# Rope by accumulating transfers, all taps of v on VectorE, and two pairs of tiles for the folded squares

## The reference

```
q, k, v = conv4(silu(xn @ Wq)), conv4(silu(xn @ Wk)), conv4(silu(xn @ Wv))   # causal, 4 taps per channel
z, a, b = xn @ Wz, xn @ Wa, xn @ Wb
q = q * cos + rot_half(q) * sin          # rot_half([u1, u2]) = [-u2, u1]; the same for k
q, k = q / |q|, k / |k|
out = sum over s in 0..3 of (q . lag(k, s)) * scale * sigmoid(lag(a, s) * b) * lag(v, s)
out = out * rsqrt(mean(out^2)) * norm_w * silu(z)
y = x + (out @ Wout) * silu(ffn(xn))     # ffn: sign weights, relu, 2048 hidden units
```

## Time and profile before

| | |
|---|---|
| time, median of 3 runs (lowest to highest) | 1356.13 us (1355.78 to 1356.19) |
| the profiled execution's own time | 1355.53 us |
| its span, first to last instruction | 1353.7 us |
| mean granted TensorE clock, as a share of full speed | 0.998 |
| busy: PE, DVE, ACT, POOL | 1318.3, 982.0, 784.5, 485.1 us |

### The profile page before, as it was taken

How to read it: one execution, slowest core, us unless ns; L and a number is a source line. 1 busy time by engine, 2 the same in 40 slices (tenths; PEclk the granted TensorE clock), 3 DMA queues, 4 the chain that set the end, 5 groups by cost and what they waited for, 6 DMA issues and landing times. The chain is left out here.

```text
span 1353.7 us, 22528 instructions
## 1 busy us (share of the span) xinstructions
PE 1318.3 (97%) x6568; PEld 1103.8 (82%) x6568; DVE 982.0 (73%) x1531; ACT 784.5 (58%) x1504; POOL 485.1 (36%) x634
## 2 busy tenths in 40 slices
PE   6999999999999999999999999999999999999998
PEld 5688888888888888888888888887888888888886
DVE  7889999999999999999999999996122223334342
ACT  5666676767766666666666676766543444422221
POOL 6245454545545455555555454553000000000001
PEclk9999999999999999999999999999999999999999
DMA  8366656666566566665666656555710101156543
GB/s 262 81 131 127 134 116 151 133 130 136 120 146 135 124 132 134 140 141 121 130 144 121 147 119 139 123 118 137 243 40 24 47 15 55 50 184 203 170 133 139
DMA packets 141562, 171.83 MB, mean 127 GB/s; under 512 B 32720, under 2 KB 69584, under 8 KB 141264
## 3 DMA queue, kind: packets, MB, share of 16 engines
q1 hardware_dynamic: 114160, 121.48, 32.0%
q0 software_dynamic: 27360, 49.82, 21.6%
HBM read 62.58 MB, written 25.30 MB: 65 GB/s over the span
## 5 line engine op out<-in xcount | busy, mean ns | idle before, releaser
L1254 DVE TENSOR_TENSOR hid_lo<-relu,hid_hi 128x512 fp32r<-128x512 f32 x64 | 44.3, 692 | 169.1 <-ACT hid_hi L1246 169.1
L798 DVE SCALAR_TENSOR_TENSOR y_k<-u_k,cw_k,y_k 128x512 f32<-128x512 f32 x192 | 146.1, 761 | 27.4 <-ACT y_k L651 20.6
L798 DVE SCALAR_TENSOR_TENSOR y_q<-u_q,cw_q,y_q 128x512 f32<-128x512 f32 x192 | 144.4, 752 | 22.5 <-ACT y_q L651 14.8
L1346 POOL TENSOR_TENSOR g_buf<-g_buf,up_raw 128x512 f32<-128x512 f32 x3 | 3.8, 1279 | 356.2 <-DVE g_buf L1406 356.2
L510 POOL TENSOR_TENSOR rnorm<-norms,neg_half 128x8 f32<-128x8 f32 x64 | 122.6, 1915 | 9.5 <-POOL norms L506 8.5
L1242 ACT ACTIVATE relu<-bank,us_sb 128x512 f32<-128x512 f32 x64 | 44.1, 690 | 123.3 <-PE bank L1265 123.3
L540 POOL DMA_DIRECT2D sq_sum<-out_sq x62 | 53.9, 869 | 162.4 <-DVE norms L831 112.4
L1366 ACT ACTIVATE hid_hi<-o_raw 128x512 fp32r<-128x512 f32 x64 | 40.2, 630 | 116.0 <-PE bank L1475 97.3
L1426 DVE TENSOR_TENSOR hid_lo<-o_raw,hid_hi 128x512 fp32r<-128x512 f32 x64 | 43.8, 690 | 79.9 <-ACT hid_hi L1366 79.9
L690 ACT ACTIVATE down_raw<-y_q 64x512 f32<-64x512 f32 x64 | 40.5, 632 | 103.3 <-PE bank L1036 103.3
L526 POOL TENSOR_TENSOR rq_win<-rq_win,const 128x32 f32<-128x32 f32 x64 | 30.1, 471 | 194.9 <-DMA rq_win<-rq_scratch 194.9
(11 more groups left out here) (193 smaller groups left out, 3711.8 us busy)
## 6 DMA issues: line engine op xcount, KB each, us to landing
swapped_q<-y_q SPq DMA_DIRECT2D x128, 128.0 KB, 2.4
swapped_k<-y_k SPq DMA_DIRECT2D x128, 128.0 KB, 2.4
o_scratch<-o_buf SPq DMA_DIRECT2D x64, 256.0 KB, 3.4
o_raw<-o_scratch SPq DMA_DIRECT2D x64, 256.0 KB, 4.0
down_raw<-down_raw POOLq DMA_DIRECT2D x63, 256.0 KB, 3.4
y_v<-down_raw POOLq DMA_DIRECT2D x63, 256.0 KB, 4.3
sq_sum<-out_sq POOLq DMA_DIRECT2D x62, 256.0 KB, 3.3
raw_q<-in_wq SPq DMA_DIRECT2D x16, 256.0 KB, 3.1
```

The source lines that it names most:

```text
L798: nc.vector.scalar_tensor_tensor(y[n][:, g % 2, :], u[n][:, g % 2, i:i + CH], cw[n][:, bass.ds(h * TAPS + i, 1)], y[n][:, g % 2, :], ALU.m ...
L1254: nc.vector.tensor_tensor(hid_lo[:, j % HS, :], relu[:, j % 2, :], hid_hi[:, j % HS, :].bitcast(fp32), ALU.subtract).then_inc(hid_lo_done, 1)
```

## The change

- **Rope.** `rope(n, i)` now has two operations instead of three. `i = 0` is `y * cos` into `rot` as before; `i = 1` multiplies `y`, not a swapped copy of it, with a sine table of opposite signs, into `swapped`. The four plain copies by SP (two each for q and k) are gone. In their place POOL's `add_swapped(n)` issues two half-height DMAs for each of q and k, which carry each half of `swapped` to the other half of `rot` and add it there. `score` waits for their landing (`rope_added`).
- **v.** The third tap of v is DVE's (line 798) in every step; ACT's last tap (line 654) and POOL's `add_last_tap` are gone, and `turn_v` waits for DVE's third tap.
- **Squares.** `fold` and `other` are two tiles each, taken by g % 2, so that ACT's squares wait for `turned_f` = c-1. POOL waits for the fold before.
- **Order.** On DVE the rope of k is one step late and stands among the taps of q; `gate_scores` and `mask_band` stand between taps 2 and 3 of k; `join_out` and `make_o` among the taps of v; the three splits are spread. On ACT silu of v comes ahead of the squares of q, and the squares of k at the end of the step. On POOL the step begins `fold_squares`, `add_swapped("q")`, `add_swapped("k")`, and then `make_gates` and the rest as before.

```
         def step(h, g):                       # POOL
             c = h * G + g
             if at := back(h, g, 1):
-                fold_squares(c)
-                add_last_tap(at[1], c)
+                fold_squares(at[1], c)
+                add_swapped("q", at[1], c - 1)
+                add_swapped("k", at[1], c - 1)
             if at := back(h, g, 3):
                 make_gates(at[1], c - 3)
...
-        def fold_squares(c):
+        def fold_squares(g1, c):
             wait(pool, squares_done, c)
+            wait(pool, folded, 16 * (c - 1))
             pool.sem_inc(fold_asked, 1)
-            nc.gpsimd.dma_start(fold, other, accum_op=ALU.add).then_inc(folded, 16)
+            nc.gpsimd.dma_start(fold[g1 % 2], other[g1 % 2], accum_op=ALU.add).then_inc(folded, 16)
+
+        def add_swapped(n, g1, k):
+            wait(pool, rope_done[n], 2 * (k + 1))
+            pool.sem_inc(rope_asked, 1)
+            for to, frm in ((0, HALF), (HALF, 0)):
+                nc.gpsimd.dma_start(rot[n][to:to + HALF, cols(g1)], swapped[n][frm:frm + HALF, g1 % 2, :],
+                                    accum_op=ALU.add).then_inc(rope_added[n][g1 % 2], 16)
...
     def step(h, g):                           # ACT
             if not is_start(h, g):
                 silu_and_tap("q", bank_qv, h, g, c)
+            if back(h, g, 4):
+                square_out(c - 4)
+            if not is_start(h, g):
                 silu_and_tap("k", bank_kz, h, g, c)
             if g == 3 and not is_last(h):
                 split_hi("q", h + 1, c)
-            squares("q", g, c)
-            if back(h, g, 4):
-                square_out(c - 4)
             silu_and_tap("v", bank_qv, h, g, c)
             if g == 3 and not is_last(h):
                 split_hi("k", h + 1, c)
-                split_hi("v", h + 1, c)
-            squares("k", g, c)
+            squares("q", g, c)
...                                            # silu of z, copy of v, save_spill
+            squares("k", g, c)
+            if g == 3 and not is_last(h):
+                split_hi("v", h + 1, c)
...
     def step(h, g):                           # DVE, after
             conv_tap("q", 1, h, g, c)
             if at1: rope("k", 0, at1[1], c - 1)
             conv_tap("q", 2, h, g, c)
             if at1: rope("k", 1, at1[1], c - 1)
             conv_tap("q", 3, h, g, c)
             conv_tap("k", 1, h, g, c)
             if at1: sum_fold(at1[1], c)
             conv_tap("k", 2, h, g, c)
             if at3: gate_scores(at3[1], c - 3); mask_band(at3[1], c - 3)
             conv_tap("k", 3, h, g, c)
             if g == 3 and not is_last(h): split_lo("q", h + 1)
             conv_tap("v", 1, h, g, c)
             rope("q", 0, g, c)
             conv_tap("v", 2, h, g, c)
             if at3: join_out(at3[1], c)
             conv_tap("v", 3, h, g, c)
             if g == 3 and not is_last(h): split_lo("k", h + 1)
             if at3: make_o(at3[0], at3[1], c - 3)
             rope("q", 1, g, c)
             if g == 3 and not is_last(h): split_lo("v", h + 1)
...
     def turn_v(g1, c):                        # PE
-            wait(pe, last_tap_added, 16 * c)
+            wait(pe, conv_done["v"], 3 * c)
...
     def score(g2, k):
-            wait(pe, rope_done["q"], 3 * (k + 1 + ahead))
-            wait(pe, rope_done["k"], 3 * (k + 1))
+            wait_rope(pe, "k", g2, k)
+            wait_rope(pe, "q", g2, k)
+            if ahead:
+                wait_rope(pe, "q", g2 + 1, k + 1)
```

More of the change, by code:

```diff
@@ L324, in attention, with wait_rope @@
     sq_asked = sem("sq_asked")
[L325 to L330, removed]
+    DVE_TAPS = {"q": 3, "k": 3, "v": 3}
+    fold, other = ([down_raw[:, i, j, :] for i in range(2)] for j in range(2))
+    def wait_rope(eng, n, g, c):
+        wait(eng, rope_added[n][g % 2], 32 * (c // 2 + 1) if isinstance(c, int) else
+             c * 16 + (32 if g % 2 == 0 else 16))
     def back(h, g, k):
@@ L570, in on_gpsimd @@
         schedule(pool, step)
+        for n in "qk":
+            add_swapped(n, G - 1, NC - 1)
         roots(H - 1, G - 1, NC)
@@ L688, in squares @@
             wait(act, conv_done[n], 3 * c + 3)
[L689 to L691 removed]
+            wait(act, turned_f, c - 1)
+            nc.scalar.activation(fold[g % 2][own, :], y[n][own, g % 2, :], ACT.Square)
+            last = nc.scalar.activation(other[g % 2][own, :], y[n][far, g % 2, :], ACT.Square)
             if n == "k":
@@ L730, in step @@
                 save_spill(at[1], c)
+            squares("k", g, c)
+            if g == 3 and not is_last(h):
+                split_hi("v", h + 1, c)
+            elif g == 3:
+                for n in "qkvz":
+                    act.wait_ge(wlo_done[n], H)
+                ffn.up_signs(0)
+                ffn.up_signs(1)
             if g == 1 and not (isinstance(h, int) and h == 0):
@@ L862, in step @@
             c = h * G + g
-            for n in "qk":
-                for i in (1, 2, 3):
-                    conv_tap(n, i, h, g, c)
+            at1, at3 = back(h, g, 1), back(h, g, 3)
+            conv_tap("q", 1, h, g, c)
+            if at1:
+                rope("k", 0, at1[1], c - 1)
+            conv_tap("q", 2, h, g, c)
+            if at1:
+                rope("k", 1, at1[1], c - 1)
+            conv_tap("q", 3, h, g, c)
+            conv_tap("k", 1, h, g, c)
+            if at1:
+                sum_fold(at1[1], c)
+            conv_tap("k", 2, h, g, c)
+            if at3:
+                gate_scores(at3[1], c - 3)
+                mask_band(at3[1], c - 3)
+            conv_tap("k", 3, h, g, c)
             if is_start(h, g):
@@ L883, in step @@
                         ALU.mult).then_inc(prod_done, 1)
[L884 to L889, removed]
+            if g == 3 and not is_last(h):
+                split_lo("q", h + 1)
+            conv_tap("v", 1, h, g, c)
             if is_start(h, g):
@@ L892, in step @@
             rope("q", 0, g, c)
[L893 to L896, removed]
             conv_tap("v", 2, h, g, c)
[L898 to L901, removed]
+            if at3:
+                join_out(at3[1], c)
+            conv_tap("v", 3, h, g, c)
             if g == 3 and not is_last(h):
                 split_lo("k", h + 1)
+            if at3:
+                make_o(at3[0], at3[1], c - 3)
+            rope("q", 1, g, c)
+            if is_end(h, g):
+                dve.wait_ge(squares_done, NC)
+                nc.vector.tensor_tensor(fold[g % 2], fold[g % 2], other[g % 2], ALU.add).then_inc(folded_last, 1)
+            if g == 3 and not is_last(h):
                 split_lo("v", h + 1)
-            for i in (1, 2):
-                rope("q", i, g, c)
-                rope("k", i, g, c)
             if is_start(h, g - 1):
```

94 lines of the change are left out of this document (39 added, 55 removed).

## The result

The changed kernel takes **1375.63 us** (median of 4 runs, 1375.57 to 1376.10) against 1355.95 for the kernel before in the same session (4 runs, 1353.48 to 1356.19): a ratio of 1.0150, with a 95% interval of 1.0132 to 1.0168. It is 1.5% slower; I had said 1351, 0.4% faster. The time lies in the stated range, but inside rival 2's 1369 to 1377 and on the other side of the kernel before from my case. The profiled execution took 1376.1, its span is 1374.3.

A forecast was written before the change was run, and what follows sets the result against it. PE, busy 97% of the span, was taken as the bound. Against 1355.5: - 16.0 (head stalls) + 13.8 (steps) - 2.0 (end) - 0.5 (start) = - 4.7, so 1350.8, stated as 1351 us; range 1336 to 1376.

The forecast's parts named there:

- rival 2: New stall outweighs gain: half-height DMA over 0.76 on POOL, 0.52 to 0.66 lost a step, 1369 to 1377; chance 0.28.
- my case: Head stalls won, PE loses 0.23 us in each step: 1351 us, 0.4% faster, spread 1346 to 1357; chance 0.43.
- d: POOL's time for one half-height DMA, bounded by 0.44 and 0.92 us, taken as 0.66; same result from 0.62 to 0.76.
- T + 11.72: Latest harmless end of mask_band in us, T being the step's start; PE loses nothing if every step meets it.
- heads and steps: Steps 3 to 62: 16.0 us of head stalls won, 60 x 0.23 = 13.8 lost to late gates.
- the start: Silu of v no longer waits in step 1; a gain of 0.5 us, since the next fold waits for other things.
- the end: Wait for silu of z (2.09) and slow clock (1.7) go, last fold and gates cost some; gain taken as 2 us.
- DVE's new order: DVE's operations timed within a step: mask_band ends at 11.61 us after its start if gates are there, 0.11 before the limit.
- the 16.0 us of the heads: Time lost in steps 3 to 62, mostly PE's sum_values waiting for coefficients once per head; all to be won.
- Three taps of v in DVE's idle time: The third tap of v on DVE costs nothing while 1.8 us are free in a step; otherwise 0.66 a step.
- a POOL operation waits for DVE's work on two tiles: POOL's third gates operation, beside tap 2 of k on DVE, waits for the tap's end and ends at 10.36 us.
- silu of v no longer waits in step 1: At the start, ACT's silu of v ahead of the squares removes a wait; taken as 0.5 us gained.

The follow-up runs named there:

- gates_first: The changed kernel with make_gates moved on POOL ahead of the half-height transfers of k: 1341.54 us, ratio to the kernel before 0.9903.
- v_two_taps: gates_first with the last tap of v left out altogether, so its output lacks that tap: 1337.73 us, ratio to the kernel before 0.9879.
- ends_too: gates_first with split_lo of k earlier on DVE, step 2's fold before step 1's key gates, third last chunk's gates before the last roots: 1336.64 us.
- three_pieces: The changed kernel with each rope half's 128 rows moved in three accumulating transfers (32, 32, 64) instead of two of 64: 1405.90 us, ratio to before 1.0385.

## Why the prediction was wrong

**The failed step** is the one that I called d, "the half-height DMA is not in the trace ... I take the middle, 0.66". It measured 0.81 (32 rows 0.77, 128 rows 0.85). The bounds 0.44 to 0.92 held it; the choice between them did not. It lies above the 0.76 from which the second gates operation also falls behind tap 2 of k, so the rest of the sum ran on rival 2's line. That line was right to a few hundredths: gates at 10.66 (measured 10.64), `gate_scores` 10.79 (10.76), `mask_band` 12.24 (12.22). Its loss per step was not as good: it said 0.52 to 0.66 with PE's draining, an ordinary step lost 0.46, and the mean over the 60 steps (34.8 us over 817.8, 0.58) lies in its span only because the heads lost 0.93, which no line of the prediction had. The draining asks for nothing on top of the distance to T + 11.72. I had two rows of 0.87 and 0.92 for full height and none lower, and took a middle that no row stood for. The Trainium skill (DMA: Bandwidth & Descriptors, Anatomy of one DMA — SWDGE (gpsimd) path) spoke for a cost that hardly depends on the number of descriptors; the three heights bear that out for POOL's share, and I had weighed it with 0.28 only.

**Size by size**, against the profiled execution: heads and steps were to give - 2.2 (- 16.0 + 13.8) and cost 18.8; the start was to give 0.5 and cost 2.7; the end was to give 2.0 and gave 1.0. The misses of 21.0, 3.2 and 1.0 make 25.2 of the 25.3 between 1350.8 and 1376.1. Of the start's 2.7, 1.4 lies ahead of step 1, and these runs cannot tell it from chance (below).

**Right**: what a step must keep (T + 11.72): steps whose `mask_band` ends at 11.63 and 11.77 take 13.63 and 13.65, one with 12.22 takes 14.09. DVE's new order, with `mask_band` at 11.61 if the gates are there: gates_first has 11.63. That the 16.0 us of the heads are to be won: with the gates in time the steps lose 1.7. Three taps of v in DVE's idle time: v_two_taps. That a POOL operation waits for DVE's work on two tiles: 0.66 beside the tap, 0.22 without it, and the Trainium skill's rule (SBUF — State Buffer, Who interferes with whom: a VectorE instruction with two SBUF inputs and a GpSimd one that reads SBUF contend) agrees. My sum had this wait in for the third operation; with the longer d it was the second that stood beside the tap, the third ran behind it in 0.23, and the wait became 0.44 of the 0.46 that a step loses.

**Off at the heads**: the first step of a head was to be like other steps; it takes 14.56, 0.46 more. Of that 0.30 comes through the gates (10.94 instead of 10.64), as tap 1 of q starts at 4.78 instead of 4.47, and rope k1 with it. The late tap is there in gates_first too (4.79), where a head costs 0.13, and with one tap fewer as well (v_two_taps, 4.78). It waits for ACT's product, which ends at 4.64 instead of 4.44, and then starts 0.14 behind it instead of 0.03. The splits are not its cause, and the trace of the changed kernel shows what it goes with: only the 13 heads that the hardware loop runs have it. The two written-out heads, which stand behind the same three splits, have their tap at 4.55 and 4.52 and take 14.23. What in the turn of the loop holds ACT and DVE is not shown.

**Off at the start**: I wrote that silu of v no longer waits in step 1 and that the next fold waits for other things anyway. The first came true and was worth more than my 0.5: step 1 takes 12.85 instead of 14.50. But the fold of step 2 waits for POOL, which stands at the key gates until DVE's table is ready (65.74, and the fold's transfer goes out at 66.94), and that hardly came earlier: 20.98 us after the start of step 1, where it had been 21.27. So PE came 1.65 earlier to a fold that was as late as before. The waits of PE before, in the stretch from 30 to 75 us:

```profile
PE bank L1036 <- DMA down_raw<-down_raw: 1.8, 1, 1.8
PE bank L968 <- ACT u_v L646: 1.7, 1, 1.7
```

The 1.7 went and the 1.8 became 2.85. Behind the 1.8 the clock had stayed at 1.00; behind the 2.85 it fell to 1.2 GHz (a mean of 0.50 from 72 to 74 us, 0.74 from 74 to 76). Step 2 takes 17.69 instead of 14.74, so steps 1 and 2 together lose 1.3. The other 1.4 of the start's 2.7 lies ahead of step 1, which begins at 45.96 here and at 44.84 in gates_first, a kernel that does not differ up to there; before, it began at 44.58. **At the end** the wait for silu of z went, with the low clock that followed it; a wait of 1.8 for `gate_scores`, behind POOL's roots, took its place, which I had named ("POOL's last gates are bounded by the late rope of k") but priced too low.

**The change as a whole** holds a gain of 13 us that one position in POOL's order turned into a loss of 20. The best version here, ends_too, is 1.3% below the kernel before and 2.8% below the changed one (1336.64 against 1375.63, in different sessions whose kernels before differ by 0.2%).

## What to carry to other kernels

An accumulating transfer that POOL issues was priced by the piece here, not by its rows (0.77 to 0.85 us for 32 to 128); when a price has to be bounded and one end is a measured neighbour, stay near that end and ask what can make the other true. In an engine's hand-written order put what the bounding engine waits for ahead of what waits for this step's late work. And where a term is quantized by another engine's instruction, look at the next step of the stairs, not only at the mean: here, by the prediction's own sum, 0.05 us past an edge of d turns a loss of 0.23 us in a step into 0.52, and 0.46 was measured.

## What the runs showed of the hardware

- POOL was held for 0.77, 0.81 and 0.85 us by an accumulating transfer of 32, 64 and 128 rows of 512 elements (the rope's of k; the squares' of 128 rows took 0.93). A following operation is recorded as started before that ends (468.94, with the transfers' end at 469.51), yet ends only behind it.
- The disturbance goes the other way too, but is small: in gates_first a rope product of DVE beside the gates took 0.71 to 0.82 instead of 0.68.
- A single idle time of 2.85 us of PE was followed by a granted clock of 0.50, and was worth 3.9 us once most of it was gone (2.27 of wait, 1.58 of clock). One of 2.09 us, in the kernel before, was followed by 0.57. Single ones of 1.8 us (before and after) and of 1.91 us (three_pieces) and 61 of up to 0.6 left the clock at 1.00.
- The first steps of the 13 heads in the hardware loop have ACT's product, and with it DVE's first tap, later than the two written-out heads do: the product by 0.12 to 0.16 us, the tap by 0.23 to 0.26 (changed kernel).
